# A two-layer graph network on one core: the turnings of x1 move from the bank of the other transpositions into the two ring banks, and every engine's order is drawn anew

## The reference

```python
# layer 0: one head of graph attention, F = 512, F1 = 256
h = X @ W                                             # (512, 256) per graph
e = leaky_relu(h @ a[0] + (h @ a[1]).T, 0.2) + NEG * (1 - adj)
x1 = layernorm(X + concat([softmax(e) @ h, h], -1))
# layer 1: attention with 8 heads of 64 features
q, k, v = (x1 @ Wq.T + bq, x1 @ Wk.T + bk, x1 @ Wv.T + bv)   # split into heads
s = where(adj == 0, -inf, q @ k.T / 8)
out = layernorm(x1 + (softmax(s) @ v) @ Wo.T + bo)
```

## Time and profile before

| | us |
|---|---|
| Median of 3 runs | 3204.15 (3191.07 to 3204.79) |
| The profiled execution | 3193.84 |
| Its span, first to last instruction | 3192.1 |
| TensorE matmuls busy | 2991.9 (94%) |
| VectorE busy | 2599.2 (81%) |
| ScalarE busy | 2462.9 (77%) |
| GpSimd busy | 2066.3 (65%) |
| Mean granted clock of TensorE, share of 2.4 GHz | 0.985 |

### The profile page before, as it was taken

How to read it: one execution, slowest core, us unless ns; L and a number is a source line. 1 busy time by engine, 2 the same in 40 slices (tenths; PEclk the granted TensorE clock), 3 DMA queues, 4 the chain that set the end, 5 groups by cost and what they waited for, 6 DMA issues and landing times.

```text
span 3192.1 us, 60592 instructions
## 1 busy us (share of the span) xinstructions
PE 2991.9 (94%) x19084; PEld 2522.3 (79%) x19084; DVE 2599.2 (81%) x6553; ACT 2462.9 (77%) x5543; POOL 2066.3 (65%) x1927
## 2 busy tenths in 40 slices
PE   5899999999999999999999999999999999999995
PEld 4788888887788887888887888887888887888874
DVE  4788888888888888888888888888888888888873
...
DMA packets 290047, 681.92 MB, mean 214 GB/s; under 512 B 40512, under 2 KB 74048, under 8 KB 256960
## 3 DMA queue, kind: packets, MB, share of 16 engines
...
## 4 chain that ended last, share of the span: by engine, by line
PE 41%; DMA 25%; ACT 13%; POOL 11%; SPq 4%; DVE 4%; issue 3%; ACTq 0%; DVEq 0%; POOLq 0%
PE R_bank L620 25%; DMA turned_lo_prob<-scratch 13%; POOL turned_lo_prob L1057 9%; PE O_bank L709 9%; DMA scratch<-blocked 8%; PE S_bank L690 5%; DMA r_wide<-r_scratch 4%; ACT turned_hi_prob L737 3%; SPq L522 2%; ACT prob L821 2%; DVE blocked L999 1%; ACT tokens L752 1%; PE L_bank L611 1%; ACT o_half L840 1%; POOL o_half L1052 1%
## 5 line engine op out<-in xcount | busy, mean ns | idle before, releaser
L1057 POOL TENSOR_TENSOR turned_lo_prob<-turned_lo_prob,turned_hi_prob 128x512 fp32r<-128x512 f32 x1024 | 1297.7, 1296 | 594.7 <-ACT turned_hi_prob L737 594.1
L999 DVE STREAM_TRANSPOSE blocked<-prob 128x512 f32<-128x512 f32 x1024 | 699.7, 698 | 167.7 <-ACT prob L821 128.9
L737 ACT ACTIVATE turned_hi_prob<-turned_lo_prob 128x512 fp32r<-128x512 f32 x1024 | 596.9, 622 | 300.6 <-DMA turned_lo_prob<-scratch 296.5
L821 ACT ACTIVATE prob<-prob,small_cols 128x512 f32<-128x512 f32 x1024 | 730.3, 715 | 68.7 <-DVE small_cols L979 67.0
L979 DVE CUSTOM_DVE_ANT_0 prob<-S_bank,mask 128x512 f32<-128x512 f32 x1024 | 674.3, 675 | 76.3 <-PE S_bank L690 72.8
L709 PE MATMUL O_bank<-turned_hi_prob,v_st 128*128 128x256 f32 x2048 | 526.8, 293 | 71.4 <-POOL turned_lo_prob L1057 65.9
L709 PE MATMUL O_bank<-turned_lo_prob,v_st 128*128 128x256 f32 x2048 | 509.7, 285 | 0.0
L709 PEld LDWEIGHTS O_bank<-turned_hi_prob,v_st 128*128 128x128 f32 x2048 | 394.4, 193 | 113.1 <-POOL turned_lo_prob L1057 86.9
L690 PE MATMUL S_bank<-qk_pair 64*128 64x512 f32 x3072 | 442.6, 413 | 16.1 <-DVE small_cols L979 15.0
L620 PE MATMUL R_bank<-wv,x1T 128*128 128x256 f32 x3072 | 413.9, 289 | 7.3 <-DVE qk_pair L896 5.5
L620 PEld LDWEIGHTS R_bank<-wv,x1T 128*128 128x128 f32 x3072 | 386.6, 193 | 25.2 <-issue 24.4
...
## 6 DMA issues: line engine op xcount, KB each, us to landing
scratch<-blocked SPq DMA_DIRECT2D x256, 1024.0 KB, 4.4
...
tokens<-xT SPq DMA_DIRECT2D x128, 256.0 KB, 5.9
tokens<-x SPq DMA_DIRECT2D x128, 256.0 KB, 4.2
r_wide<-r_scratch SPq DMA_DIRECT2D x512, 64.0 KB, 3.7
out<-tokens SPq DMA_DIRECT2D x128, 256.0 KB, 4.3
r_scratch<-r_cols SPq DMA_DIRECT2D x256, 2.0 KB
...
```

The costliest lines, as they stand in the source:

```text
L737: act.activation(dst, src, ACT.Copy).then_inc(done, 1)
L821: act.activation(prob_tile(R, s), prob_tile(R, s), ACT.Exp, bias=negmax[:, slot:slot + 1], scale=-1.0, accum_out=psum_row[:, ph % 2, j:j + ...
L999: dve.transpose(blocked[:, ph % 2, :, :, 2 * (s % 2) + s % 4 // 2, :].rearrange("p d c i -> p c d i"), prob_tile(R, s).rearrange("p (c d i ...
L1057: pool.tensor_tensor(turned_lo_prob[:, ph % 2, a, :, :], turned_lo_prob[:, ph % 2, a, :, :].bitcast(F32), turned_hi_prob[:, a, :, :].bitca ...
```

## The change

Two things change. First, `E0` to `E3` leave `SOLO` and become uses of the ring: they write an `R_bank`, count `ring_mm` when written and `ring_done` when emptied, and have a semaphore `x1_hi` of their own between ScalarE and VectorE. Whoever waited for `solo_done` of an E now waits for `ring_done`. The ring has 28 uses in a turn instead of 24, and `L_bank` serves only `B`, `C` and `N`. Second, all the lists are drawn anew. Nothing is added or taken away from what is computed; instructions and their shapes stay the same. In the diff some lines of `VECTOR_PLAN` are left out, and the lists `PROLOGUE` and `ENDING`, where the order of `ENDING` on each single engine stays as it was.

```diff
@@ -53,95 +53,95 @@
 TENSOR_PLAN = (
     "k1 N weigh",
     "weigh scores scores",
-    "O0 O1 O2",
-    "C0 scores scores",
+    "C0 O0 O1",
+    "O2 scores scores",
     "weigh weigh O3",
     "q2 k2 C1",
     "weigh D0 weigh",
-    "scores scores A3",
-    "D1 W0 W1",
-    "C2 W2 W3",
-    "weigh C3 D2",
-    "weigh scores scores",
-    "D3 q3 k3",
-    "weigh weigh E0",
-    "scores scores E1",
-    "scores E2 V0",
-    "V1 E3 weigh",
-    "weigh B0 scores",
-    "q4 k4 weigh",
-    "weigh B1 V2",
-    "scores scores V3",
-    "scores B2 weigh",
-    "weigh q1 B3",
+    "scores scores D1",
+    "C2 W0 W1",
+    "scores W2 W3",
+    "C3 D2 weigh",
+    "weigh scores D3",
+    "q3 k3 weigh",
+    "weigh E0 E1",
+    "scores scores E2",
+    "V0 V1 E3",
+    "B0 weigh weigh",
+    "scores q4 scores",
+    "k4 weigh weigh",
+    "A3 B1 V2",
+    "scores V3 scores",
+    "B2 q1 weigh",
+    "weigh scores B3",
     "scores",
 )
 SCALAR_PLAN = (
-    "evQ1 exp exp lows",
-    "N turn pre0 hi",
-    "exp hi aexp0 hi",
-    "hi exp exp pre1",
-    "exp C0 exp hi",
-    "hi hi hi aexp1",
-    "lows exp exp evQ2",
-    "pre2 exp turn aexp2",
-    "C1 fin0 hi exp",
-    "hi hi evW0 hi",
-    "fin1 evW1 lows pre3",
-    "C2 evW2 exp aexp3",
-    "evW3 fin2 exp exp",
-    "C3 turn fin3 hi",
-    "exp hi hi hi",
-    "lows A0 exp exp",
-    "exp evQ3 lap0 lap1",
-    "turn E0 lap2 hi",
-    "E1 hi hi exp",
-    "lows hi E2 lap3",
-    "exp exp E3 exp",
-    "turn evV0 evV1 hi",
-    "lows hi hi exp",
-    "hi A1 B0 exp",
-    "exp evQ4 exp turn",
-    "A2 hi hi hi",
-    "B1 lows hi exp",
-    "evV2 exp evV3 exp",
-    "B2 A3 turn exp",
-    "lows hi hi hi",
-    "B3 hi exp exp",
+    "evQ1 N exp pre0",
+    "exp lows aexp0 turn",
+    "exp exp hi pre1",
+    "hi hi exp hi",
+    "C0 exp exp hi",
+    "hi hi aexp1 hi",
+    "exp lows exp exp",
+    "evQ2 turn pre2 C1",
+    "aexp2 fin0 hi hi",
+    "hi lows pre3 C2",
+    "evW0 exp evW1 exp",
+    "hi aexp3 evW2 exp",
+    "evW3 turn exp C3",
+    "fin1 hi lows hi",
+    "hi A0 hi exp",
+    "exp fin2 fin3 exp",
+    "evQ3 exp lap0 lap1",
+    "lap2 E0 turn E1",
+    "hi hi E2 hi",
+    "exp evV0 lap3 hi",
+    "lows exp evV1 E3",
+    "exp exp turn A1",
+    "hi hi hi hi",
+    "exp lows B0 exp",
+    "exp exp evQ4 A2",
+    "B1 turn hi hi",
+    "evV2 lows hi hi",
+    "exp exp exp evV3",
+    "A3 B2 turn exp",
+    "hi lows hi hi",
+    "hi B3 exp exp",
     "turn",
 )
 VECTOR_PLAN = (
...
-    "lrs sum vt vt",
-    "evQ3 vt E0 reduce",
-    "reduce inv E1 reduce",
-    "vt reduce E2 sum",
-    "vt vt E3 vt",
-    "evV0 evV1 inv reduce",
...
+    "reduce vt vt reduce",
+    "evQ1 red0 sum vt",
+    "vt reduce reduce inv",
+    "vt reduce reduce evO0",
+    "vt yst0 evO1 vt",
+    "C0 inv red1 evO2",
...
+    "evW3 C3 evD2 vt",
+    "reduce reduce reduce evD3",
+    "lst2 lst3 vt sum",
+    "lrs reduce vt vt",
+    "evQ3 vt inv E0",
+    "E1 reduce reduce reduce",
+    "E2 evV0 vt sum",
+    "reduce evV1 E3 vt",
+    "vt vt reduce reduce",
+    "inv vt reduce sum",
+    "reduce B0 vt vt",
+    "vt evQ4 inv B1",
+    "evV2 reduce reduce reduce",
...
 GPSIMD_PLAN = (
@@ -151,62 +151,62 @@
     "lo lo",
     "lo lo",
     "norm yrs",
+    "turn lo",
     "lo lo",
-    "turn lo",
     "lo norm",
     "turn lo",
     "lo lo",
     "lo lrs",
-    "norm turn",
+    "A0 norm",
+    "turn lo",
+    "lo lo",
+    "lo norm",
+    "turn A1",
     "lo lo",
     "lo lo",
-    "A0 norm",
     "bo0 bo1",
+    "bo2 norm",
+    "turn A2",
+    "lo lo",
+    "lo lo",
+    "norm A3",
     "turn lo",
+    "lo norm",
     "lo lo",
-    "lo A1",
-    "norm turn",
-    "A2 lo",
-    "lo lo",
-    "lo norm",
-    "turn A3",
-    "norm lo",
-    "lo lo",
-    "lo bo2",
-    "turn bo3",
+    "bo3 turn",
 )
 SP_PLAN = (
     "mv sv",
-    "rl mv",
-    "rs sv",
-    "mv sv",
-    "rs fin0",
-    "rl fin1",
-    "mv xt0",
-    "fin2 xt1",
-    "sv rs",
-    "rl mv",
-    "sv fin3",
     "rs rl",
     "mv sv",
-    "rl xt2",
-    "ld0 rs",
-    "mv ld1",
-    "sv xt3",
+    "rs mv",
+    "sv rl",
+    "fin0 mv",
+    "rs xt0",
+    "rl sv",
+    "fin1 fin2",
+    "mv sv",
+    "rl rs",
+    "fin3 xt1",
+    "mv xt2",
+    "xt3 rl",
+    "sv ld0",
+    "ld1 rs",
+    "mv sv",
     "rl ld2",
     "rs mv",
+    "rs ld3",
+    "rl sv",
     "rl rs",
-    "ld3 sv",
-    "rs rl",
 )
-START = "A0 A1 B0 w0 A2 B1 w1 A3 B2 B3"
...
+START = "A0 A1 B0 w0 A2 B1 A3 B2 w1 B3"
...
@@ -223,7 +223,7 @@
-    return [name for name in " ".join(plan).split() if parse(name)[0] in ("q", "k", "V", "W", "O", "D")]
+    return [name for name in " ".join(plan).split() if parse(name)[0] in ("q", "k", "V", "W", "O", "D", "E")]
 FIRST_LAYER = ring_uses([PROLOGUE])
@@ -236,7 +236,7 @@
 RING0 = len(FIRST_LAYER) + len(FIRST_ROUND) - len(ROUND)
-SOLO = ["B0", "B1", "B2", "B3", "C0", "C1", "C2", "C3", "E0", "E1", "E2", "E3"]
+SOLO = ["B0", "B1", "B2", "B3", "C0", "C1", "C2", "C3"]
 class Round:
@@ -389,7 +389,7 @@
         h_lo, terms_ready = sem("h_lo"), sem("terms_ready")
         n_mm, n_copied = sem("n_mm"), sem("n_copied")
         a_pre, a_red, a_exp, a_inv = sem("a_pre"), sem("a_red"), sem("a_exp"), sem("a_inv")
-        x1_ready, bo_added = sem("x1_ready"), sem("bo_added")
+        x1_ready, x1_hi, bo_added = sem("x1_ready"), sem("x1_hi"), sem("bo_added")
         ln_dve = [sem(f"ln_dve{i}") for i in range(2)]
         ln_pool = [sem(f"ln_pool{i}") for i in range(2)]
         wa_done = sem("wa_done")
@@ -606,10 +606,10 @@
                     pe.wait_ge(solo_done, before)
                 return solo_bank(name)
-            def solo_turn(bank, src):
+            def turn(bank, src, done):
                 for c in range(4):
                     last = pe.transpose(bank[:, c * P:(c + 1) * P], src[:, c * P:(c + 1) * P], ident[:, :])
-                last.then_inc(solo_mm, 1)
+                last.then_inc(done, 1)
             def project(dst, stationary, moving, done, last_chunk=None):
@@ -641,18 +641,19 @@
                         pe.wait_ge(n_copied, R.nx(1, 1))
                     if i == T - 1:
                         pe.wait_ge(a_pre, R.nx(4, T))
-                    solo_turn(solo(R, name), alpha[:, :])
+                    turn(solo(R, name), alpha[:, :], solo_mm)
                 if kind == "D":
                     out_b = ring(R, name)
                     pe.wait_ge(solo_done, solo_count(R, f"C{i}"))
                     project(out_b[:, 0:F1], lambda s, c: turned[:, s, c, :], lambda m, c: h0[:, m, c, :],
                             ring_mm)
                 if kind == "E":
+                    out_b = ring(R, name)
                     pe.wait_ge(x1_ready, R.nx(4, i + 1))
-                    solo_turn(solo(R, name), tokens[R.buffer(1)][:, i, :])
+                    turn(out_b, tokens[R.buffer(1)][:, i, :], ring_mm)
                 if kind in ("q", "k"):
                     if name == "q4":
-                        pe.wait_ge(solo_done, solo_count(R, "E3"))
+                        pe.wait_ge(ring_done, R.ring("E3", 1))
                     c0, w = (i % 4) * P, wq if kind == "q" else wk
                     project(ring(R, name)[:, :], lambda s, c: w[:, s, c, c0:c0 + P], lambda m, c: x1T[:, m, c, :],
                             ring_mm)
@@ -660,7 +661,7 @@
                     if R.prologue and i == 0:
                         pe.wait_ge(w_lo, 4)
                     if kind == "V":
-                        pe.wait_ge(solo_done, solo_count(R, f"E{i}"))
+                        pe.wait_ge(ring_done, R.ring(f"E{i}", 1))
                     c0 = 0 if kind == "V" else D // 2
                     project(ring(R, name)[:, 0:D // 2], lambda s, c: x1T[:, s, c, i * P:(i + 1) * P],
                             lambda m, c: wv[:, m, c, c0:c0 + D // 2], ring_mm)
@@ -788,10 +789,10 @@
                     act.wait_ge(ln_pool[0], R.nx(2, 2))
                     layer_apply(R, 0, 1, i, x1_ready)
                 if kind == "E":
-                    act.wait_ge(solo_mm, solo_count(R, name))
+                    act.wait_ge(ring_mm, R.ring(name, 1))
                     if i == 0 and not R.prologue:
                         act.wait_ge(ring_mm, R.ring("k3", 1))
-                    split_hi(x1T[:, HI, :, i * P:(i + 1) * P], solo_bank(name)[:, :].rearrange("p (c t) -> p c t", c=C), solo_hi)
+                    split_hi(x1T[:, HI, :, i * P:(i + 1) * P], R_bank[R.bank(name)][:, :].rearrange("p (c t) -> p c t", c=C), x1_hi)
                 if kind == "w":
                     act.wait_ge(w_loaded[1 + i], 16)
                     place = (tokens[2][:, :, :], stage().rearrange("p (c n) -> p c n", c=C))[i % 2]
@@ -936,9 +937,9 @@
                 if kind == "lrs":
                     layer_scales(0, lambda c: R.nx(10, c))
                 if kind == "E":
-                    dve.wait_ge(solo_hi, solo_hi_count(R, name))
-                    split_lo(x1T[:, LO, :, i * P:(i + 1) * P], solo_bank(name)[:, :].rearrange("p (c t) -> p c t", c=C),
```

(71 more changed lines are left out.)

## The result

The changed kernel takes 3244.31 us (median of 4 runs, 3238.64 to 3246.7) against 3202.16 us for the kernel before; the ratio is 1.0136, with a 95% interval from 1.0108 to 1.0164. It is slower by 42 us, where 21 us less had been forecast, and it lies outside the stated range.

A forecast was written before the change was run, and what follows sets the result against it. TensorE was taken as the bound; idle time of 1.75 + 0.75 + 0.3 = 2.8 us a graph instead of 3.5 saves 20 us over 30.2 graphs, the prologue 1: 3204 - 21 = 3183 us, range 3133 to 3224.

The forecast's parts named there:

- What bounds the kernel: Whole kernel: TensorE is the bound, busy 2775.0 of 2880 us; its 105 us idle are all another order could win.
- the sum: Per graph: stalls of 1.75, 0.75 and 0.3 add to 2.8 us of TensorE idle time instead of 3.5.
- The turnings: From k3 to E3: stalls of 0.4, 0.2, 0.2 and 0.95 us, 1.75 a graph against 1.9 before.
- E0's 0.4: First turning after k3: E0 stalls 0.4 us for ScalarE's layer apply lap0, which stands behind exp23.
- V1's 0.95: V1 takes E2's bank and stalls 0.95 us, as three reductions on VectorE stand ahead of E2's low part.
- rival 3: Phase 4 loads late behind fin1, fin2; hi16, then E2 late, paid at V1; at 2.5 us late 3229 us; chance 0.15.
- rival 1: Phase 5 loads 1 us or more late behind fin3, xt1; weigh 10 stalls, turnings' gain gone; about 3205 us; chance 0.22.
- Weigh 10: The weigh after the turnings: low part at K+21.3 (K is k3's end), TensorE at K+21.6; no stall.
- Weigh 12 and weigh -2: Later weighs: all weigh stalls fall from 1.1 to about 0.3 us a graph; weigh -2's low part 0.3 us late.
- C0: After k1, in O0's old place: C0 waits for aexp0 and stalls 0.75 us, swallowing weigh -2's 0.3.
- TensorE's work is the same: Whole graph: shapes and counts stay, so nothing is gained or lost but TensorE's idle time.

The follow-up runs named there:

- pairs: The changed kernel with three pairs of scores units joined again on TensorE (10 with 11, 14 with 15, 16 with 17): 3246.41 us, ratio 1.0136.
- e2_first: The changed kernel with E2 on ScalarE put ahead of hi16 and hi17, which wait for their DMA: 3242.3 us, ratio 1.0128.
- before_xt_small: The kernel before with the loads of x transposed cut to 32 of 512 columns from the first full turn on: 3173.54 us, ratio 0.9908.
- fin2_later: The changed kernel, on SP alone the store fin2 moved from ahead of the loads of phase 4 to behind them: 3217.59 us, ratio 1.0053.
- fin2_tail: fin2_later with the end of a graph redrawn on ScalarE, VectorE, GpSimd and SP (among others rl6 ahead of ld3): 3205.86 us, ratio 1.0015.
- tail_1011: fin2_tail with scores 10 joined with 11 on TensorE: 3206.05 us, ratio 1.0015.
- the three last runs: fin2_tail with scores 10 and 11 joined, with C0 behind O2 (pre1, red1 moved along), or both: 3206.05, 3218.69 and 3219.25 us.

## Why the prediction was wrong

*What bounds the kernel.* "All that another order could win" was read from TensorE's idle time, and TensorE taken as the pace everywhere. The step that failed is the sum, 2.8 us of idle time a graph instead of 3.5: measured are 4.2, and 0.8 us more of busy time. Three things are in this. The busy time is answered below. The sum added TensorE's stalls as if each were worth its length, but from weigh 7 to weigh 10 and from weigh 11 to weigh -2 the loops through memory set the pace of the changed kernel, as `pairs` and `e2_first` show. In the kernel before it is the second loop alone: weigh -2 starts right behind its low part there too, but weigh 10 hardly stalls, and what `before_xt_small` gains comes in part by the turnings. And two terms were put at next to nothing: what fin2 does to the loads of phase 4 and the store of phase 5 (26 us by `fin2_later`), and the lateness of weigh -2 (12 us by `fin2_tail`).

*The turnings.* E0's 0.4 was right. V1's 0.95 was right for the mechanism named, the three reductions: once fin2 is out of the way V1 stalls 0.75 in the graph shown for `fin2_later`:

```profile
1606.03 1.67 PE L620 MATMUL R_bank<-wv,x1T 128*128 128x256 f32 x12 [0.75 <-DVE x1T L879]
```

In the changed kernel it is 1.52 by rival 3's mechanism: hi16 idles for its DMA ahead of E2, because fin2 holds up the loads of phase 4. Rival 3 named the queue, the instruction and the activation, and was given 0.15 on the ground that the store of phase 4 would be issued about 1 us earlier. It went at K-7.29, not earlier but 0.3 us later than in the kernel before (means of 28 graphs, K-7.62 there), and the loads at K-1.84 where they had gone at K-2.5. In the kernel before nothing that waits so late for ScalarE stands ahead of these loads. What the rival had wrong is the payment: not at V1, which the waits behind it absorb (`e2_first`), but through the store of phase 5, which then takes 6.1 us to its loads where the kernel before has 5.0 and I had allowed 0.3 more. That is rival 1's chain with rival 3's cause.

*Weigh 10* was forecast at K+21.6 and starts at K+22.3 in the graph shown, K+22.7 on average. Two terms of its chain were wrong. The store of phase 5 was to go at K+2.3, because VectorE would have vt21 and vt22 done; but vt23 waits for weigh 7, and the store goes at K+2.75, where it went before at K+2.9. This wait is also what closes the loop, and the prediction doesn't have it. And the 19.22 us from the store to weigh 10 (19.04 in the new order) were carried over from one graph of the old order, though the distance between store and loads depends on the queue: the mean is 19.9.

*Weigh 12 and weigh -2.* Weigh 12's stall went, as said. Weigh -2's lateness, put at 0.3 and counted as swallowed by C0, is 1.37 us a graph, the second largest stall. Its order was read rightly (rl6 behind ld3, norm6 between the low parts), and undoing it gives 0.36 us of that loop back; the size was off.

*C0.* Right in place; stall and weigh -2 together were to be 0.75 and are 1.37 + 0.19.

*TensorE's work is the same.* The instructions are, but they take 93.4 us a graph against 92.6, and "nothing is gained or lost but idle time" was wrong by about half of what a graph lost. A scores unit alone takes 0.89 from start to next start and half a pair 0.79, and a V before a unit takes 1.62 for 1.53; the new order has eight units alone, the old four. But `pairs` and `tail_1011` don't turn this into time: inside the loops the idle time takes its place, between weigh -2 and weigh 6 the wait for a ring bank does. With fin2 and the end of a graph put right (`fin2_tail`, windows view from 170 to 3050 us) TensorE idles 3.2 us a graph, 0.3 less than in the kernel before and half of what was promised, and is busy 93.3: level, and no more.

*Left open.* 0.25 us a graph between weigh -2 and weigh 6 and 0.24 in the second loop of `fin2_tail`, against the kernel before; the three last runs don't place them. Open too is why the store of phase 5 lands so late behind late loads. A version of `fin2_tail` with fin1 and fin3 moved as well was not tried.
